# Gated delta-rule layer on one core: unnormalised keys and queries, with their sums of squares as token columns

## The chip, the cores and the metric

The kernel runs on one core of a Trainium2 chip. The core has TensorE (PE; its weight loads are shown as PEld), VectorE (DVE), ScalarE (ACT), GpSimd (POOL) and SyncE (SP), which starts the transfers. The metric is the device time of one execution in microseconds (us), less is better.

## The reference

Two layers work on 4 x 256 tokens of width 256: rotary attention with a routed feed-forward part (layer 0), then a gated delta rule with another feed-forward part (layer 1). The change lies in the delta rule. It has 16 key heads and 32 value heads (two value heads share a key head) of width 128:

```python
conv = sum((w[None, :, j:j + 1] * padded[:, :, j:j + T] for j in range(K)))
conv = jax.nn.silu(conv)
...
q = _l2norm(q)          # a / max(sqrt(sum(a*a)), 1e-12)
kk = _l2norm(kk)
beta = jax.nn.sigmoid(b_raw)
g = -jnp.exp(A_log) * jax.nn.softplus(a_raw + dt_bias)
decay = jnp.exp(g)
def step(state, inp):
    state = state * d_t[..., None, None]
    Sk = jnp.einsum('bhi,bhij->bhj', k_t, state)
    delta = (v_t - Sk) * b_t[..., None]
    state = state + jnp.einsum('bhi,bhj->bhij', k_t, delta)
    o = jnp.einsum('bhi,bhij->bhj', q_t, state)
...
y = o * jax.nn.silu(zz)
y = y * jax.lax.rsqrt(jnp.mean(y * y, axis=-1, keepdims=True) + 1e-06) * norm_w
out = jnp.einsum('btv,ov->bto', y.reshape(B, T, VDIM), W_out)
```

The kernel returns the residual stream after both layers.

## The kernel before

Everything is laid out by hand: each engine has its own program, and semaphores join them. Tokens are cut into 8 tiles of 128; a batch row has 256 tokens, two chunks of 128. Layer 1 starts with a norm, the decays' sums, the whole feed-forward part (`up`, `down`) and the preparation of head 0. Then `body(j, slot, i)` runs once for each of 16 key heads: heads 0, 1, 14 and 15 are written out and the rest is a loop of two heads. Within a body an engine works on head i and, in gaps that the lists `fill`, `mid`, `end` and `more` name, prepares head i + 1 and finishes the output of head i - 1.

One head goes through these stages.

- Products. TensorE turns V to token rows (`turn_v`, L764), ScalarE copies it (`copy_v`), GpSimd makes `Rb`, the bf16 copy of V's first chunk, in the first place of its body (`vb_done`, L1635). TensorE makes K K^T and K Q^T of every batch row (`products`, L777, L778). VectorE multiplies K K^T by the strict mask and by the decays (`matrices`, L1339, L1344, result N); ScalarE copies K Q^T (`copy_qk`, L1126) and GpSimd multiplies it by the decays (`decayed`, L1629). With them run z's gate (`tanh_z`, `gate_z`) and the sum of squares of the output of head i - 1 (`square_y`, `sum_y`, `mean_y`, then ScalarE's `scale_y`, Ln and Exp, L1169 and L1171), by which GpSimd scales y (`scale_y`, L1621).
- Inversion. ScalarE copies N to bf16 (Nb, L1132), TensorE turns TT (L815), and ScalarE copies the result (d_T, L1137). Then six levels (`LEVELS`) double the size of the inverted blocks: `corner` (L790), a masked copy by VectorE (L1363), `grow` (L800, L804), ScalarE's copies (L1145, L1149). Between them TensorE projects head i + 1 (`project`, L731), turns y (`turn_y`, L886) and projects the output (`project_out`, L897), and VectorE makes the convolution in steps of 128 x 1024 (`conv`, L1311). GpSimd adds the diagonal to N (L1649) and the mask to the next decays (`mask`, L1615).
- Solve. For two chunks c and three rounds a: `apply` (L840), `residual` (L852) or `link` (L860) on TensorE, `left_over` (L1377) and `update` (L1385) on VectorE.
- Output. `outputs` (L873 to L875), then `gate_o` (L1408).

Keys and queries of head i + 1 are normalised during the solve: ScalarE squares them (`square`), TensorE sums over the 128 partitions with a matrix of ones, so that the sum of a token stands in all partitions of a bank (`norms`, L751, banks 0 to 3), VectorE bounds it from below into `nrm` (`guard`, L1329, which increments `max_done`), ScalarE takes the power -1/2 as Ln and Exp (`rnorm`, L1096 and L1098), and VectorE multiplies (`unit`, L1335, which increments `kq_done`). `project_z` (L742) waits for `max_done`, since z's projection takes the same banks, and `products` waits for `kq_done`. `ACT_TABLE_LOAD` is put in by the compiler where ScalarE's next function is in another table.

## Time and profile before

| what | value |
|---|---|
| median of 3 runs | 1980.0 us (1975.21 to 1981.11) |
| profiled execution: time, span | 1971.39 us, 1969.4 us |
| busy: TensorE, VectorE, ScalarE, GpSimd | 89%, 77%, 62%, 32% |
| chain that ended last | PE 39%, DVE 12%, ACT 10%, issue 9%, POOL 2% |
| costliest group on VectorE | L1311, 192 instructions, 298.1 us |

The span is the time from the first to the last instruction of one profiled execution. Busy shares are shares of the span. The chain is followed back from the last instruction, at each step to what released it; the rest of it is time in between. Where a line of a timeline ends in brackets, the engine sat idle for so long before it, and the name is what released it.

### The profile page before, as it was taken

The page shows a single profiled execution, that of the slowest core. Times are in us where ns is not written, and L with a number is a line of the kernel's source. Part 1 is how long each engine was busy: PE and PEld are TensorE (multiplying, and loading weights), DVE is VectorE, ACT ScalarE, POOL GpSimd, SP SyncE. Part 2 cuts the span into 40 slices and gives each one's busy share as a digit, 9 for nine tenths or more (in the row PEclk, how much of TensorE's full clock was granted, in tenths as well). Part 3 has the DMA queues.
Part 4 walks back from the last instruction along what each step waited for, and adds up shares of the span by engine and source line. Part 5 has one row for each costly group of instructions (what it writes and reads, how often), then busy time and mean ns, then how long its engine had stood idle before and what let it go on. Part 6 is the DMA issues. An engine that isn't in the chain of part 4 may idle for free.

```text
span 1969.4 us, 35372 instructions
## 1 busy us (share of the span) xinstructions
PE 1749.0 (89%) x12824; PEld 1303.0 (66%) x12824; DVE 1519.3 (77%) x2421; ACT 1226.4 (62%) x2155; POOL 636.4 (32%) x442
## 2 busy tenths in 40 slices
PE   7899999999899778889888889888988888988976
PEld 5667676767657566667766667666776666756665
DVE  8788888888674787887777878778777787877853
ACT  3253534444355567777677877768767786777862
POOL 2212222231230535336053261432605326144140
PEclk9999999999999899999999999999999999999988
DMA  3011110101032001101101011010110101101000
GB/s 131 32 62 38 54 61 31 61 31 62 3 99 65 17 16 39 33 23 33 56 23 33 23 34 55 23 34 23 33 55 23 33 23 34 55 23 33 7 1 22
DMA packets 51465, 75.66 MB, mean 38 GB/s; under 512 B 3392, under 2 KB 41792, under 8 KB 51184
## 3 DMA queue, kind: packets, MB, share of 16 engines
q1 hardware_dynamic: 51312, 73.55, 11.7%
q8 instruction: 105, 1.72, 0.4%
q14 instruction: 48, 0.39, 0.1%
HBM read 72.29 MB, written 1.25 MB: 37 GB/s over the span
## 4 chain that ended last, share of the span: by engine, by line
PE 39%; DVE 12%; ACT 10%; issue 9%; POOL 2%; ACTq 0%; DVEq 0%; POOLq 0%
PE bank L897 6%; PE bank L731 6%; PE bank L852 5%; PE bank L742 4%; DVE d_sil L1311 4%; PE bank L790 2%; DVE d_Rb L1377 2%; PE bank L800 2%; PE bank L764 2%; POOL d_dec L1629 2%; DVE d_W L1385 2%; PE bank L873 1%; PE bank L875 1%; PE bank L874 1%; ACT d_TT L1149 1%
## 5 line engine op out<-in xcount | busy, mean ns | idle before, releaser
L1311 DVE SCALAR_TENSOR_TENSOR d_sil<-d_pre,d_w,d_sil 128x1024 f32<-128x1024 f32 x192 | 298.1, 1553 | 5.9 <-ACT d_pre L1081 5.6
L1635 POOL TENSOR_TENSOR d_Rb<-d_V,d_ones 128x512 bf16<-128x512 f32 x32 | 48.0, 1511 | 711.0 <-ACT d_V L1110 711.0
L1363 DVE CAST_PREDICATED d_X<-tables_sb,bank 128x512 bf16<-128x512 int32 x192 | 134.3, 700 | 147.6 <-PE bank L790 146.9
L731 PE MATMUL bank<-xnT,d_w 128*128 128x512 f32 x480 | 244.1, 644 | 0.8
L189 PE MATMUL bank<-xnT,a_w 128*128 128x512 f32 x512 | 237.0, 597 | 0.0
L1145 ACT ACTIVATE d_T<-bank 128x512 bf16<-128x512 f32 x160 | 98.5, 616 | 107.4 <-PE bank L800 105.1
L1629 POOL TENSOR_TENSOR d_dec<-d_dec,d_qk 128x384 f32<-128x384 f32 x128 | 133.2, 1064 | 44.2 <-DVE d_N L1344 44.2
L852 PEld LDWEIGHTS bank<-d_W,d_N 128*128 128x128 f32 x1024 | 122.7, 193 | 35.0 <-DVE d_W L1385 22.4
L189 PEld LDWEIGHTS bank<-xnT,a_w 128*128 128x128 f32 x512 | 90.9, 192 | 78.5 <-issue 78.5
L731 PEld LDWEIGHTS bank<-xnT,d_w 128*128 128x128 f32 x480 | 89.2, 202 | 79.3 <-issue 79.3
L489 POOL TENSOR_TENSOR a_hidc<-a_hid,a_comb 128x512 f32<-128x512 f32 x32 | 44.4, 1387 | 295.0 <-DVE a_hid L336 295.0
L852 PE MATMUL bank<-d_W,d_N 128*128 128x128 f32 x1024 | 129.6, 280 | 11.1 <-DVE d_W L1385 9.6
L742 PE MATMUL bank<-d_w,xnT 128*128 128x256 f32 x512 | 123.4, 384 | 12.0 <-DVE d_nrm L1329 12.0
L1377 DVE TENSOR_TENSOR d_Rb<-d_V,bank 128x512 bf16<-128x512 f32 x128 | 86.5, 685 | 56.9 <-PE bank L852 55.8
L897 PE MATMUL bank<-d_wo,d_yT 128*128 128x256 f32 x512 | 127.8, 394 | 0.9 <-ACT d_yT L1176 0.9
L508 ACT ACTIVATE a_sg<-a_sm 128x384 f32<-128x384 f32 x64 | 33.0, 515 | 151.9 <-DVE a_sm L341 151.9
L790 PE MATMUL bank<-d_T,d_Nb 128*128 128x64 bf16 x1536 | 79.2, 196 | 48.0 <-ACT d_T L1137 33.7
L1615 POOL TENSOR_TENSOR d_dec<-d_dec,tables_sb 128x512 f32<-128x512 f32 x64 | 116.6, 1850 | 16.2 <-DMA d_dec<-decay_scratch 16.2
L1649 POOL TENSOR_TENSOR d_N<-d_N,tables_sb 128x512 f32<-128x512 f32 x64 | 120.3, 1910 | 0.0
L1149 ACT ACTIVATE d_TT<-bank 128x512 bf16<-128x512 f32 x192 | 117.4, 611 | 4.5 <-PE bank L804 4.5
L790 PEld LDWEIGHTS bank<-d_T,d_Nb 128*128 128x128 bf16 x1536 | 65.0, 100 | 81.3 <-ACT d_T L1137 36.4
L481 POOL TENSOR_TENSOR a_qT<-a_rot_a,a_rot_b 128x512 f32<-128x512 f32 x64 | 81.2, 1270 | 100.4 <-DVE a_rot_b L325 100.4
(211 smaller groups left out, 4497.9 us busy)
## 6 DMA issues: line engine op xcount, KB each, us to landing
d_dec<-decay_scratch SPq DMA_DIRECT2D x32, 512.0 KB, 5.7
a_w<-w SPq DMA_DIRECT2D x16, 897.0 KB, 4.6
d_w<-w SPq DMA_DIRECT2D x16, 776.0 KB, 4.8
a_comb<-comb_scratch SPq DMA_DIRECT2D x16, 512.0 KB, 5.5
d_dec<-decay_scratch SPq DMA_DIRECT2D x32, 256.0 KB, 6.0
d_wo<-w SPq DMA_DIRECT2D x16, 256.0 KB, 3.0
f_w<-w SPq DMA_DIRECT2D x8, 256.0 KB, 3.7
tables_sb<-tables SPq DMA_DIRECT2D x1, 1056.0 KB, 8.4
```

Source lines behind the costliest of these rows:

```text
L189: last = pe.matmul(psum[bank][:, :], wq(slot, part, k), xnT[:, k, half * HALF:(half + 1) * HALF], start=(k == 0), stop=(k == KT - 1))
L731: last = pe.matmul(psum[bank][:, :], cols(slot, (c * KT + k) * P, P), xnT[:, k, h * HALF:(h + 1) * HALF], start=(k == 0), stop=(k == KT - 1))
L742: last = pe.matmul(psum[n][:, q * 2 * P:(q + 1) * 2 * P], xnT[:, k, t * P:(t + 1) * P], cols(slot, OZ + k * 2 * P, 2 * P), start=(k == 0), ...
L790: last = pe.matmul(psum[4 + 2 * v][:, n * 64:(n + 1) * 64], Nb[v][:, n // 2, n % 2, :], left(Tm[v][:, :, :], lv)[:, n], start=True, stop=True)
L852: last = pe.matmul(psum[5 + 2 * v][:, b * P:(b + 1) * P], N[v][:, b, 2 * c, :], Wv[v][:, b, c, :], start=True, stop=True)
L897: last = pe.matmul(psum[OUT_BANK[n]][:, q * D:(q + 1) * D], yT[v][:, t * P:(t + 1) * P], wo[slot][:, v, :], start=(v == 0), stop=(v == 1))
L1149: act.activation(right(TT[v][:, :, :], lv).rearrange("p n g w -> p (n g) w"), psum[4 + 2 * v][:, :].rearrange("p (a w) -> p a w", w=lv), A ...
L1311: dve.scalar_tensor_tensor(sil[c][:, :, :], pre[c % 2][:, :, tap:tap + S], cols(slot, OC + 4 * c + tap, 1), sil[c][:, :, :], ALU.mult, ALU ...
L1363: dve.copy_predicated(left(Xp[lv][:, v], lv), mask.unsqueeze(1).broadcast_to([P, 8, 64]).rearrange("p n (g w) -> p n g w", w=lv), psum[4 + ...
L1377: dve.tensor_tensor(Rb[v][:, :, :], V[v][:, :, c, :], psum[5 + 2 * v][:, :].rearrange("p (b d) -> p b d", b=B), ALU.add).then_inc(s["r_don ...
L1629: pool.tensor_tensor(g, g, qk[b % 2][:, :, :], ALU.mult).then_inc(s["p_done"], 1)
L1649: last = pool.tensor_tensor(n, n, tabs["neg_ident"].unsqueeze(1).broadcast_to([P, B, P]), ALU.add)
```

## The change

Keys and queries keep their length. With k = |k| k', the system for delta is the same when the columns of N and of the decayed K Q^T are divided by |k|^2 and V is multiplied by |k|; the length of q only scales the output, which a norm follows, so it goes into that norm's epsilon.

- The squares (`sq`) are now the stationary operand and one column of ones the moving one: 16 matmuls of one output column, all into bank 2, so a token's sum stands in its own partition.
- `guard` makes three columns of 8: `kss` (bounded sum of k), `qeps` (16e-6 times the bounded sum of q) and `krec`, the reciprocal of `kss`. It stands once in `end[3]`. `rnorm` and `unit` are gone. `key_norm`, a Sqrt on 8 columns, stands behind the last `copy_qk`.
- `copy_qk` and the first instruction of `matrices` are cut in two, for each chunk of keys has its own column of `krec`.
- GpSimd makes `Rb` as V times |k| and scales V in place, both behind `decayed(3)`; `apply` and the first `left_over` wait for them.
- `mean_y` adds `qeps` in place of 16e-6. `scale_y` on ScalarE becomes `root_y` (Sqrt), and the reciprocal, `inverse_y`, is VectorE's, behind `gate_z(3)` in level 0.

```diff
@@ -576,7 +576,11 @@
         gated = [m.sb(f"d_gated{h}", [P, 4, 2 * P]) for h in range(2)]
-        nrm = [m.sb(f"d_nrm{k}", [P, T]) for k in range(2)]
+        sq = [m.sb(f"d_sq{k}", [P, T]) for k in range(2)]
+        kss = m.sb("d_kss", [P, NT])
+        knorm = m.sb("d_knorm", [P, NT])
+        krec = m.sb("d_krec", [P, NT])
+        qeps = [m.sb(f"d_qeps{k}", [P, NT]) for k in range(2)]
         Xp = {lv: m.sb(f"d_X{lv}", [P, 2, 8, P], BF16) for lv in LEVELS}
...
@@ -733,7 +737,13 @@
             def project_z(slot, i, n):
-                pe.wait_ge(s["max_done"], i * 2 + n // 2 + 1)
+                if n < 2:
+                    pe.wait_ge(s["pre_done"], i * 8 + 5 + n)
+                    need(pe, s["acc_done"], (i - 2) * 4 + 3 + n)
+                elif n == 2:
+                    pe.wait_ge(s["kss_done"], i * 2 + 2)
+                else:
+                    pe.wait_ge(s["pre_done"], i * 8 + 8)
                 if isinstance(i, int) and i == 0 and n >= 2:
...
@@ -744,12 +754,14 @@
             def norms(i, c, h):
+
                 pe.wait_ge(s["sq_done"], i * 2 + c + 1)
-                pe.wait_ge(s["pre_done"], i * 8 + 4 + 2 * c + h + 1)
-                if c == 0:
-                    need(pe, s["acc_done"], (i - 2) * 4 + 2 + h + 1)
-                pe.matmul(psum[2 * c + h][:, :], onesf[:, :], nrm[c][:, h * HALF:(h + 1) * HALF],
-                          start=True, stop=True).then_inc(s["ssq_ready"], 1)
+                pe.wait_ge(s["pre_done"], i * 8 + 7)
+                for t in range(4 * h, 4 * h + 4):
+                    last = pe.matmul(psum[2][:, c * NT + t:c * NT + t + 1], sq[c][:, t * P:(t + 1) * P], onesf[:, 0:1],
+                                     start=True, stop=True)
+                if h:
+                    last.then_inc(s["ssq_ready"], 1)
...
@@ -831,7 +843,7 @@
                     pe.wait_ge(s["tt_done"], i * 12 + 11 + v)
-                    pe.wait_ge(s["vb_done"], i * 2 + v + 1)
+                    pe.wait_ge(s["vb_done"], i * 4 + 2 * v + 1)
                 elif k == 3:
...
@@ -902,7 +914,7 @@
                 project_z(slot, i, 2)
-                pe.wait_ge(s["kq_done"], i * 2 + 2)
+                pe.wait_ge(s["sil_done"], i * 4 + 2)
                 products(i, 0)
...
@@ -1035,12 +1036,13 @@
             down(2)
+            pe.wait_ge(ev["first_done"], 1)
             for h in range(2):
-                first_norms(0, h)
+                norms(0, 0, h)
             up(4)
             down(3)
             for h in range(2):
-                first_norms(1, h)
+                norms(0, 1, h)
             for u in range(5, UNITS):
...
@@ -1051,7 +1053,8 @@
                 else:
-                    pe.wait_ge(s["max_done"], 2)
+                    pe.wait_ge(s["kss_done"], 2)
+                    pe.wait_ge(s["pre_done"], 8)
                 for r in range(2):
...
@@ -1088,14 +1091,13 @@
                 act.wait_ge(s["sil_done"], i * 4 + c + 1)
-                act.activation(nrm[c][:, :], sil[c][:, :, :].rearrange("p b t -> p (b t)"), ACT.Square).then_inc(s["sq_done"], 1)
-
-            def rnorm(i, c):
-
-                act.wait_ge(s["max_done"], i * 2 + c + 1)
-                act.activation(nrm[c][:, :], nrm[c][:, :], ACT.Ln).then_inc(s["ln_done"], 1)
-                act.wait_ge(s["ln_done"], i * 2 + c + 1)
-                act.activation(nrm[c][:, :], nrm[c][:, :], ACT.Exp, scale=-0.5).then_inc(s["nrm_done"], 1)
+                act.activation(sq[c][:, :], sil[c][:, :, :].rearrange("p b t -> p (b t)"), ACT.Square).then_inc(s["sq_done"], 1)
+
+            def key_norm(i):
+
+                act.wait_ge(s["kss_done"], i * 2 + 1)
+                need(act, s["vb_done"], i * 4)
+                act.activation(knorm[:, :], kss[:, :], ACT.Sqrt).then_inc(s["knorm_done"], 1)
...
@@ -1123,8 +1125,11 @@
                     act.wait_ge(s["p_done"], i * 8 + 2 * (b - 2) + 2)
-                act.activation(qk[b % 2][:, :, :], psum[5 + 2 * (b % 2)][:, 0:3 * P].rearrange("p (c t) -> p c t", c=3),
-                               ACT.Copy).then_inc(s["qk_done"], 1)
+                act.wait_ge(s["krec_done"], i + 1)
+                ps = psum[5 + 2 * (b % 2)][:, 0:3 * P].rearrange("p (c t) -> p c t", c=3)
+                act.activation(qk[b % 2][:, 0:2, :], ps[:, 0:2, :], ACT.Copy, scale=krec[:, 2 * b:2 * b + 1])
+                act.activation(qk[b % 2][:, 2, :], ps[:, 2, :], ACT.Copy,
+                               scale=krec[:, 2 * b + 1:2 * b + 2]).then_inc(s["qk_done"], 1)
...
@@ -1164,11 +1169,9 @@
-            def scale_y(i):
+            def root_y(i):
                 act.wait_ge(s["yssm_done"], i + 1)
-                act.activation(yss[:, :, :], yss[:, :, :], ACT.Ln).then_inc(s["ysqrt_ln"], 1)
-                act.wait_ge(s["ysqrt_ln"], i + 1)
-                act.activation(yrs[:, :, :], yss[:, :, :], ACT.Exp, scale=-0.5).then_inc(s["yrs_done"], 1)
+                act.activation(yss[:, :, :], yss[:, :, :], ACT.Sqrt).then_inc(s["ystd_done"], 1)
...
@@ -1199,8 +1202,9 @@
                 copy_qk(i, 3)
+                key_norm(i)
                 if not first:
-                    scale_y(i - 1)
+                    root_y(i - 1)
                 fill = [([], []) for _ in LEVELS]
...
@@ -1233,8 +1237,6 @@
                     batch_decays(ni, ns, 3)
-                    rnorm(ni, 0)
-                    rnorm(ni, 1)
...
@@ -1322,22 +1322,24 @@
-            def guard(i, c, bank=0):
-                for h in range(2):
-                    dve.wait_ge(s["ssq_ready"], i * 4 + 2 * c + h + 1)
-
-                    last = dve.tensor_scalar(nrm[c][:, h * HALF:(h + 1) * HALF], psum[(bank or 2 * c) + h][:, :], 4e-24, None, ALU.max)
-                last.then_inc(s["max_done"], 1)
-
-            def unit(i, c):
-                dve.wait_ge(s["nrm_done"], i * 2 + c + 1)
-                f = sil[c][:, :, :].rearrange("p b t -> p (b t)")
-                dve.tensor_tensor(f, f, nrm[c][:, :], ALU.mult).then_inc(s["kq_done"], 1)
+            def guard(slot, i):
+                dve.wait_ge(s["ssq_ready"], i * 2 + 2)
+                need(dve, s["knorm_done"], i)
+                dve.tensor_scalar(kss[:, :], psum[2][:, NT:2 * NT], 4e-24, None, ALU.max).then_inc(s["kss_done"], 1)
+                dve.tensor_scalar(qeps[slot][:, :], psum[2][:, 0:NT], 4e-24, 16e-6, ALU.max, ALU.mult).then_inc(s["kss_done"], 1)
+                dve.wait_ge(s["kss_done"], i * 2 + 1)
+                need(dve, s["qk_done"], i * 4)
+                dve.reciprocal(krec[:, :], kss[:, :]).then_inc(s["krec_done"], 1)
             def matrices(i, slot, b):
                 dve.wait_ge(s["kk_ready"], i * 4 + b + 1)
-                dve.tensor_tensor(kk[b % 2][:, :, :], psum[4 + 2 * (b % 2)][:, 0:3 * P].rearrange("p (c t) -> p c t", c=3),
-                                  tabs["strict3"].rearrange("p (c t) -> p c t", c=3), ALU.mult).then_inc(s["kk_done"], 1)
+                dve.wait_ge(s["krec_done"], i + 1)
+                ps = psum[4 + 2 * (b % 2)][:, 0:3 * P].rearrange("p (c t) -> p c t", c=3)
+                strict = tabs["strict3"].rearrange("p (c t) -> p c t", c=3)
+                dve.scalar_tensor_tensor(kk[b % 2][:, 0:2, :], ps[:, 0:2, :], krec[:, 2 * b:2 * b + 1], strict[:, 0:2, :],
+                                         ALU.mult, ALU.mult)
+                dve.scalar_tensor_tensor(kk[b % 2][:, 2, :], ps[:, 2, :], krec[:, 2 * b + 1:2 * b + 2], strict[:, 2, :],
+                                         ALU.mult, ALU.mult).then_inc(s["kk_done"], 1)
                 dve.wait_ge(s["kk_done"], i * 4 + b + 1)
...
@@ -1374,6 +1376,8 @@
                 dve.wait_ge(s["resid_ready"], i * 10 + 2 * k + v + 1)
+                if c == 0 and a == 0:
+                    dve.wait_ge(s["vb_done"], i * 4 + 2 * v + 2)
                 dve.tensor_tensor(Rb[v][:, :, :], V[v][:, :, c, :], psum[5 + 2 * v][:, :].rearrange("p (b d) -> p b d", b=B),
...
@@ -1413,10 +1417,15 @@
-            def mean_y(i):
+            def mean_y(slot, i):
                 dve.wait_ge(s["yss_done"], i * 2 + 2)
-                dve.tensor_scalar(yss[:, :, :], yss[:, :, :], 1.0 / P, 16e-6, ALU.mult, ALU.add).then_inc(s["yssm_done"], 1)
+                dve.scalar_tensor_tensor(yss[:, :, :], yss[:, :, :], 1.0 / P, qeps[slot][:, :].unsqueeze(1).broadcast_to([P, 2, NT]),
+                                         ALU.mult, ALU.add).then_inc(s["yssm_done"], 1)
+
+            def inverse_y(i):
+                dve.wait_ge(s["ystd_done"], i + 1)
+                dve.reciprocal(yrs[:, :, :], yss[:, :, :]).then_inc(s["yrs_done"], 1)
...
@@ -1455,16 +1464,17 @@
                 if not first:
-                    mean_y(i - 1)
+                    mean_y(1 - slot, i - 1)
                 matrices(i, slot, 3)
                 fill = [([], []) for _ in LEVELS]
                 mid, end = [[] for _ in range(6)], [[] for _ in range(6)]
                 fill[0][0].append(lambda: gate_z(i, 3))
+                if not first:
+                    fill[0][0].append(lambda: inverse_y(i - 1))
                 if nxt:
                     nj, ns, ni = nxt
                     cv = lambda c, *steps: (lambda: conv(ns, ni, c, steps))
                     si = lambda c: (lambda: silu(ni, c))
-                    gd = lambda c: (lambda: guard(ni, c))
                     fill[0][0].append(lambda: columns(nj, ns, ni))
...
@@ -1477,9 +1487,8 @@
                     mid[2], end[2] = [cv(3, 1)], [cv(3, 2)]
-                    mid[3], end[3] = [si(2)], [gd(0)]
-                    mid[4], end[4] = [si(3)], [gd(1)]
-                    mid[5] = [lambda: unit(ni, 0)]
+                    mid[3], end[3] = [si(2)], [lambda: guard(ns, ni)]
+                    mid[4] = [si(3)]
                 if first:
...
@@ -1510,7 +1519,6 @@
                         plain(v)
-                    unit(ni, 1)
...
@@ -1600,7 +1605,8 @@
                 sum_y(LAST, v)
-            mean_y(LAST)
+            mean_y(LAST % 2, LAST)
+            inverse_y(LAST)
             for n in range(4):
...
@@ -1630,10 +1636,6 @@
                 nxt = after(j, slot, i)
-                for v in range(2):
-                    pool.wait_ge(s["v_done"], i * 4 + 2 * v + 2)
-                    pool.tensor_tensor(Rb[v][:, :, :], V[v][:, :, 0, :], onesf[:, :].unsqueeze(1).broadcast_to([P, B, P]),
-                                       ALU.mult).then_inc(s["vb_done"], 1)
                 decayed(i, slot, 0)
...
@@ -1641,6 +1643,13 @@
                 decayed(i, slot, 3)
+                pool.wait_ge(s["knorm_done"], i + 1)
+                scale = knorm[:, :].rearrange("p (b c) -> p b c", c=2).unsqueeze(3).broadcast_to([P, B, 2, P])
+                for v in range(2):
+                    pool.wait_ge(s["v_done"], i * 4 + 2 * v + 2)
+                    pool.tensor_tensor(Rb[v][:, :, :], V[v][:, :, 0, :], scale[:, :, 0, :], ALU.mult).then_inc(s["vb_done"], 1)
+                    pool.wait_ge(s["vb_done"], i * 4 + 2 * v + 1)
+                    pool.tensor_tensor(V[v][:, :, :, :], V[v][:, :, :, :], scale, ALU.mult).then_inc(s["vb_done"], 1)
                 for v in range(2):
                     pool.wait_ge(s["nb_done"], i * 2 + v + 1)
                     pool.wait_ge(s["tt1_done"], i * 2 + v + 1)
```

## Rows read from the trace of the kernel before

**Rows 1.** The page: busy time, share of the span and instructions of each engine.

```profile
PE 1749.0 (89%) x12824; PEld 1303.0 (66%) x12824; DVE 1519.3 (77%) x2421; ACT 1226.4 (62%) x2155; POOL 636.4 (32%) x442
```

**Rows 2.** Timeline of TensorE in one head: start, us, instructions, idle time before.

```profile
1239.84 0.41 PE L790 MATMUL bank<-d_T,d_Nb 128*128 128x64 bf16 x8 [2.32 <-ACT d_T L1137]
...
1241.94 3.64 PE L731 MATMUL bank<-xnT,d_w 128*128 128x512 f32 x4
...
1247.57 1.07 PE L886 MATMUL bank<-tables_sb,x_sb 128*128 128x128 f32 x8
...
1251.98 1.95 PE L731 MATMUL bank<-xnT,d_w 128*128 128x512 f32 x4
...
1269.66 0.40 PE L840 MATMUL bank<-d_Rb,d_TT 128*128 128x128 bf16 x4 [0.47 <-ACT d_TT L1149]
...
1271.67 1.95 PE L852 MATMUL bank<-d_W,d_N 128*128 128x128 f32 x16
...
1278.08 1.02 PE L751 MATMUL bank<-d_nrm,d_ones 128*128 128x512 f32 x2
...
1289.14 1.99 PE L742 MATMUL bank<-d_w,xnT 128*128 128x256 f32 x8 [0.80 <-DVE d_nrm L1329]
...
1290.97 1.95 PE L852 MATMUL bank<-d_W,d_N 128*128 128x128 f32 x16
```

**Rows 3.** Waits from 640 to 1900 us: who waited for whom, total, times, longest.

```profile
PE bank L742 <- DVE d_nrm L1329: 12.0, 15, 0.8
```

**Rows 4.** Timeline of VectorE in the same head.

```profile
1252.60 2.39 DVE L1311 SCALAR_TENSOR_TENSOR d_sil<-d_pre,d_w,d_sil 128x1024 f32<-128x1024 f32 x1
...
1276.65 1.28 DVE L1311 SCALAR_TENSOR_TENSOR d_sil<-d_pre,d_w,d_sil 128x1024 f32<-128x1024 f32 x1
...
1287.80 1.28 DVE L1329 TENSOR_SCALAR d_nrm<-bank 128x512 f32<-128x512 f32 x2
```

**Rows 5.** Groups by line, whole span: shapes, count, busy us, mean ns, idle before.

```profile
L1096 ACT ACT_TABLE_LOAD x32 | 41.1, 1283 | 0.6
...
L1096 ACT ACTIVATE d_nrm<-d_nrm 128x1024 f32<-128x1024 f32 x32 | 33.8, 1057 | 0.4
...
L1118 ACT ACTIVATE d_dec<-d_dec,d_gcol 128x256 f32<-128x256 f32 (+1 forms) x256 | 94.4, 442 | 0.0
...
L1126 ACT ACTIVATE d_qk<-bank 128x384 f32<-128x384 f32 x64 | 31.0, 485 | 29.5 <-POOL d_dec L1629 27.3 <-PE bank L778 2.2
...
L1419 DVE TENSOR_SCALAR d_yss<-d_yss 128x16 f32<-128x16 f32 x16 | 2.7, 166 | 0.0
...
L1621 POOL TENSOR_TENSOR x_sb<-x_sb,d_yrs 128x1024 f32<-128x1024 f32 x32 | 60.4, 1906 | 101.1 <-ACT d_yrs L1171 101.1
```

**Rows 6.** The router's matmuls, L309: durations min/median/max, first and last start.

```profile
L309 PE MATMUL bank<-r_w,xnT x32: 173/256/256, 19.8 to 23.2; 128*128 128x8 f32 x32
```

**Rows 7.** Timeline of ScalarE in the same head.

```profile
1232.37 0.49 ACT L1126 ACTIVATE d_qk<-bank 128x384 f32<-128x384 f32 x1 [1.72 <-POOL d_dec L1629]
...
1235.82 1.99 ACT L1132 ACTIVATE d_Nb<-d_N 128x1024 bf16<-128x1024 f32 x2
...
1266.57 1.06 ACT L1086 ACTIVATE d_yT<-d_sil 128x1024 f32<-128x1024 f32 x1 [1.02 <-PE bank L897]
```

**Rows 8.** Timeline of ScalarE behind the last head.

```profile
1944.25 1.28 ACT L1169 ACT_TABLE_LOAD   x1
...
1945.72 0.22 ACT L1169 ACTIVATE d_yss<-d_yss 128x16 f32<-128x16 f32 x1 [0.19 <-DVE d_yss L1419]
```

**Rows 9.** Timeline of GpSimd in the same head, and in the last head.

```profile
1243.54 7.91 POOL L1649 TENSOR_TENSOR d_N<-d_N,tables_sb 128x512 f32<-128x512 f32 x4
...
1251.41 6.93 POOL L1615 TENSOR_TENSOR d_dec<-d_dec,tables_sb 128x512 f32<-128x512 f32 x4
...
1896.85 4.98 POOL L1649 TENSOR_TENSOR d_N<-d_N,tables_sb 128x512 f32<-128x512 f32 x4
```

**Rows 10.** A stretch: length, busy us by engine, granted clock, DMA share, GB/s.

```profile
1242.00:1244.00 2.00, 2.00 (x7) 0.97 (x4) 2.00 (x3) 0.73 (x2) 2.00 (x3) 0.50 0.00 0
```

24 lines of the change are left out of this document (5 added, 19 removed).

## The prediction

> **What bounds the kernel.** I read the page first, then the groups by line, the waits, and the timelines of one steady head of layer 1 engine by engine. TensorE is busy 89% of the span [rows 1], so a saving on another engine counts only where TensorE stands still for it. Everything the change touches lies in layer 1 with its 16 heads. In the timeline of one head the reader is to see three kinds of stretch. In most of the inversion TensorE runs on, and other engines' work is free. At the start of the inversion ScalarE is the last link: the first product waits 2.32 us for the copy of d_T [rows 2]. In the solve VectorE and TensorE answer each other, and one wait there belongs to the normalisation: z's projection waits 0.80 us for the guard [rows 2], in 15 heads, 12.0 us in all [rows 3].
>
> **Solve stage, per head.** Four guards and two products with the norm leave VectorE: two pairs of 1.28, as the one at 1287.80, and two instructions on 1024 columns, each about a convolution step alone, 1.28 [rows 4], 5.1 us. Most of it buys nothing. The products with the norm fall before the last gating and after `plain`, where VectorE would only wait for TensorE. The first guard pair is what z's projection waits for. Three instructions on 8 columns replace it. The nearest row is `mean_y` on 16 columns, 166 ns [rows 5], so some 0.4 us, and the projection no longer waits for them: banks 0 and 1 hold no sums any more. TensorE gains its whole wait, 0.80 us. The next lateness is TensorE itself: projection and residual follow one another, 1289.14 and 1290.97 [rows 2], so the second guard's end gives nothing. TensorE's norms: before, four fp32 matmuls of 512 columns, two records each, one such pair 1.02 us from start to end at 1278.08 [rows 2], up to 4 us per head. Now 16 of one column, 32 records. The router's 32 records of 8 columns ran from 19.8 to 23.2 [rows 6], 0.11 us each, so 3.5 us: equal. Three of the four calls lie where TensorE waits for VectorE or ScalarE anyway. The bounds are -0.1 and +0.3 us; I take 0.
>
> **ScalarE.** Out go two Ln/Exp pairs on 1024 columns, each instruction 1057 ns and each behind a table load of 1283 ns [rows 5]: 9.4 us per head, at the very end of the head, after which ScalarE waited for TensorE: 0 on the path. `scale_y` is different. It lies between `copy_qk` and the Nb copy. From the end of `copy_qk` at 1232.86 to Nb at 1235.82 are 2.96 us [rows 7], two loads and two small instructions. Now one load (Sqrt) serves `key_norm` and `root_y`: 1.28 and two small ones of (2.96 - 2.57) / 2 = 0.2, 1.7 us, a gain of 1.25. Against it: `copy_qk` is cut in two with a scale column. The nearest pair, 256 and 128 columns in the decays with a mean of 442, against 485 for one [rows 5], gives +0.40 at most; with the overlap of neighbours I take +0.3. VectorE's `matrices` is cut likewise. A cut adds the fixed part of one instruction, at most `mean_y`'s 166 ns [rows 5]; I take +0.13. Two of these stand before the last `copy_qk` (it waits for `decayed(1)`, that for N): +0.26 and its own +0.3. The gain is 1.25 - 0.56 = 0.7 us per head (bounds 0 and 1.25). The transposes behind the projections come some 0.4 us later, still before the d_T copy wants them.
>
> After Sqrt, Tanh needs its table again: a load of 1.28 in front of `tanh_in` in level 5. At the end of the kernel the load starts at 1944.25, although its activation waited until 1945.72 for VectorE [rows 8]: a load does not wait for the semaphore. Before L1086 ScalarE was idle 1.02 us [rows 7]. So 0.27 us are exposed, passed on through d_TT to `apply`; the whole 1.28 is the upper bound. The Trainium skill (ScalarE: Activation LUTs, What ACT_TABLE_LOAD costs) adds a drain of 1.38 us to every load; the rows show none, as two loads fit in the gap before Nb. By the page the load saved would be worth 2.66 and the forecast about 20 us lower, unless the load added in level 5 takes that back.
>
> **GpSimd** loses its place in time. `vb_done` leaves the start of the head, where it ran under other work, and comes back behind `decayed(3)` with the scaling of V, 1024 columns in place, twice, beside it. The broadcast along the last axis is `scale_y`'s, 1.9 us for 1024 [rows 5]; so 2 x (1.5 + 1.9) = 6.8 us. Also `yrs` is now made by a VectorE reciprocal behind the first copy of level 0 and the gating. It is ready at about 1241 instead of before Nb at 1235.8, 5 us later. `decayed(2)`, `decayed(3)`, the diagonal and the mask shift by 5 + 6.8, some 12 us: the diagonal's end from 1251.4 to about 1263, the mask's from 1258.3 to about 1270 [rows 9]. The residual wants the diagonal at 1271.67 [rows 2], 1270 when TensorE has gained, and ScalarE the mask at about 1273. Slack 7 and 3 us: nothing waits. `turn_y` at 1247.57 [rows 2] needs the first scaled half and gets it at about 1244: also free. VectorE's reciprocal is one small instruction.
>
> The shared cost is another. The convolution step takes 2.39 us at 1252.60, beside GpSimd's mask, and 1.28 at 1276.65, alone [rows 4]; the diagonal's four took 7.91 us there and 4.98 in the last head, which has no convolutions [rows 9]. The scaling of y ran in a hole of VectorE and now falls on convolutions, and the mask comes up to the solve. In most of this time TensorE is the bound; I take +0.3 us per head (bounds 0 and +2). The Trainium skill (GPSIMD Engine Reference, Specifications) says that the two engines share the SBUF interface, with contention for VectorE instructions with two SBUF inputs. The rows agree, and this is the rule that speaks against the change.
>
> **Clock.** After TensorE's short idle times at the start of the inversion the granted clock was 0.50 from 1242 to 1244, the lower level, 1.2 GHz [rows 10]; four records of L731 took 3.64 us there and 1.95 at full clock [rows 2]: 1.7 us lost. Eight heads of the inversion show this; the others have about the same idle time at full clock, so it is at the edge. The 2.32 us shrink by 0.7 + 0.4 to about 1.2. I expect most falls to go: 5 of 8, 8 us. Bounds: all go, 13 us gained; or all 15 heads fall, 12 us lost.
>
> **Sum.** Per head -0.80 - 0.7 + 0.27 + 0.3 = -0.93; over 15 heads -14. Head 0 has no `scale_y` and so pays a load and the longer pieces, +2. The tail saves one load and has a reciprocal instead of Exp, -1.2. Before the heads TensorE is full and the norms cost the same, 0; the clock -8. Together -21. The profiled execution took 1971.4 us (span 1969.4 and 2.0 around it), which becomes 1950. It lies 8.6 below the median of the runs, 1980.0; the change of -21 set against that median gives 1959.
>
> **Rivals.** A, nothing gained: the table load is exposed in full, and the split pieces cost their upper bounds. Then -0.80 - 0.5 + 1.28 + 0.3 = +0.3 per head, 4 in all, and the clock brings back some 5: 1980. For it: TensorE already waits 0.47 us for d_TT at `apply` [rows 2]. Against: the early load [rows 8]. B, the other side: GpSimd becomes the bound. Its work from y's scaling to the first half of the diagonal must fit in 29 us (1241 to 1270). Uncontended that is 3.8 + 3.9 + 2.6 + 3.8 + 2.5 = 16.6; all slowed by 7.91 / 4.98 = 1.6, 26; if scaling V goes at the mask's rate, 6.93 / 4 for 512 columns [rows 9], 29. From there the residual waits, and the mask runs into the solve, where VectorE paces TensorE: two convolutions 1.1 slower each, +2.2, and a wait of up to 1; with 1.2 gained elsewhere +2 per head, +30, 2010. C: the removed VectorE and ScalarE work counts more, half of the 5.1 us: -2.6 more per head, 1920; the idle time that follows it speaks against this.
>
> **Chances.** Forecast case 0.73, A 0.13, B 0.10, C 0.04. A measurement here can tell 0.3%, 6 us, from no change. The forecast case runs from 1943 (clock all gained, no contention) to 1976 (clock unchanged, contention 0.8 per head) and leaves about 0.04 within 0.3%; A gives mostly same. Faster 0.73, same 0.14, slower 0.13. The range for 8 in 10 is 1942 to 1984, A included.
>
> **What would show it.** Right: no wait of L742 for VectorE in the solve; two table loads per head instead of six; Nb 1.2 us nearer to the end of `copy_qk`; the wait for d_T at the start of the inversion under 1.6 us; fewer L731 groups above 3 us. Wrong: TensorE or ScalarE waiting for d_N, d_dec or x_sb from GpSimd; convolutions above 2 us inside the solve; a wait for d_TT above 1 us at `apply`.

## The result and the profile after

The changed kernel takes 1997.0 us (median of 4 runs, 1992.6 to 2000.3) against 1977.6 us for the kernel before in the same session (1971.0 to 1981.1): ratio 1.0102, 95% interval 1.0077 to 1.0128. The forecast was 1959, with 0.73 on faster: it is slower, outside the range, and by none of the rivals. The profiled execution spans 1990.3 us where that of before spans 1969.4, 20.9 more. Runs 3 and 12 below had one execution each far above their others (2982 and 2462 us), which the ranges given leave out.

The page of the changed kernel, to be read beside [rows 1]:

```profile
PE 1778.5 (89%) x13208; PEld 1379.0 (69%) x13208; DVE 1488.4 (75%) x2453; ACT 1089.6 (55%) x2090; POOL 730.2 (37%) x474
...
PE 43%; DVE 13%; ACT 9%; issue 7%; DVEq 0%; POOL 0%; ACTq 0%; POOLq 0%
```

VectorE lost 31 us of work and ScalarE 137, as the diff says. GpSimd gained 94. TensorE did the same matrix products, apart from the sums, and is busy 30 us longer. The same work in more time points at its clock (mean granted clock 0.952 here, 0.971 before).

Where it went is found by cutting each head at five starts in TensorE's timeline: V is turned (L776, before L764), TT is turned (L827, L815), first product of the inversion (L802, L790), first `apply` (L852, L840), first product of the output (L885, L873). Means over heads 1 to 14, in us; the last column is from one head's start to the next:

| kernel | products | TT to first product | inversion | solve | head |
|---|---|---|---|---|---|
| before | 16.60 | 3.36 | 28.41 | 26.91 | 81.49 |
| after | 16.92 | 2.36 | 29.44 | 28.18 | 83.08 |
| difference | +0.32 | -1.00 | +1.03 | +1.27 | +1.59 |

Fourteen heads make +22 of the 21 us; head 0 pays 0.7 more with its lead, the last head with the tail gives 2.0 back.

A head's stage has one length at full clock and a longer one when the clock falls in it, and the two are easily told apart: in the kernel before the inversion takes 27.5 in six of these heads and 28.9 to 30.0 in the other eight, and the products 16.03, or 17.6 to 17.7 in five heads, all where the loop of two heads begins a new turn. In the changed kernel the products take 16.46, or 18.1 in four heads, the inversion 28.70 once and 29.3 to 29.9 in 13 heads, and all 14 solves take 27.6 us or more (one 31.4), with a stretch at the lower clock in each. Timeline of TensorE in one solve of the changed kernel, and the windows over it (length, busy us by engine, granted clock, DMA share, GB/s):

```profile
1290.33 1.01 PE L761 MATMUL bank<-d_ones,d_sq 128*128 128x1 f32 x8
1291.88 2.05 PE L864 MATMUL bank<-d_W,d_N 128*128 128x128 f32 x16 [0.55 <-DVE d_W L1389]
1293.77 0.95 PE L761 MATMUL bank<-d_ones,d_sq 128*128 128x1 f32 x8
1294.58 0.69 PE L852 MATMUL bank<-d_Rb,d_TT 128*128 128x128 bf16 x8
1295.11 1.00 PE L761 MATMUL bank<-d_ones,d_sq 128*128 128x1 f32 x8
1296.67 3.68 PE L872 MATMUL bank<-d_W,d_N 128*128 128x128 f32 x16 [0.55 <-DVE d_W L1389]
```

```profile
1292.00:1296.00 4.00, 4.00 (x40) 3.92 (x40) 4.00 (x6) 2.35 (x6) 0.00 (x0) 1.00 0.00 0
1296.00:1300.00 4.00, 3.45 (x18) 3.36 (x18) 3.10 (x5) 0.67 (x2) 0.00 (x0) 0.60 0.02 4
```

The reader is to see that `link` (L872) takes 3.68 us for the sixteen matmuls for which `residual` (L864) takes 2.05, and that the granted clock, at 1.00 until then, averages 0.60 there: most of these 4 us lie at the lower level, 1.2 GHz. `link` is the longer one in 13 of the 14 heads; in one (solve 27.6) the low stretch lies beside it. What TensorE did just before is three groups of the new sums, 128 x 1. By group, whole span:

```profile
L761 PE MATMUL bank<-d_ones,d_sq 128*128 128x1 f32 x512 | 68.4, 255 | 0.3 <-ACT d_sq L1094 0.3
L872 PE MATMUL bank<-d_W,d_N 128*128 128x128 f32 x256 | 54.0, 397 | 10.3 <-DVE d_W L1389 10.2
```

In the kernel before the group that answers to L872 has the same count and a mean of 289 ns instead of 397.

ScalarE and VectorE at the end of the inversion, and the product that follows on TensorE:

```profile
1281.03 1.28 ACT L1089 ACT_TABLE_LOAD   x1 [1.00 <-PE bank L909]
1282.33 1.06 ACT L1089 ACTIVATE d_yT<-d_sil 128x1024 f32<-128x1024 f32 x1
...
1284.72 0.58 ACT L1154 ACTIVATE d_TT<-bank 128x512 bf16<-128x512 f32 x1
```

```profile
1283.42 4.00 DVE L1317 SCALAR_TENSOR_TENSOR d_sil<-d_yT,d_sil 128x1024 f32<-128x1024 f32 x2 [0.47 <-ACT d_yT L1089]
```

```profile
1254.40 0.41 PE L802 MATMUL bank<-d_T,d_Nb 128*128 128x64 bf16 x8 [1.31 <-ACT d_T L1142]
...
1257.01 3.06 PE L735 MATMUL bank<-xnT,d_w 128*128 128x512 f32 x4
...
1285.36 0.40 PE L852 MATMUL bank<-d_Rb,d_TT 128*128 128x128 bf16 x4 [1.03 <-ACT d_TT L1154]
```

The new table load started only after ScalarE's idle time behind L909, not in it, and the second `apply` waits 1.03 us for d_TT, which stood behind the load; it was 0.47 before [rows 2]. The wait at the start of the inversion fell from 2.32 [rows 2] to 1.31, yet the projection behind it took 3.06 us for four records, 1.95 at full clock [rows 2]. So it was in the other heads: 16 loads at L1089, with 14.3 us of idle time before them. And GpSimd in the same head:

```profile
1256.51 4.73 POOL L1627 TENSOR_TENSOR x_sb<-x_sb,d_yrs 128x1024 f32<-128x1024 f32 x2 [8.70 <-DVE d_yrs L1428]
...
1268.16 2.76 POOL L1652 TENSOR_TENSOR d_V<-d_V,d_knorm 128x1024 f32<-128x1024 f32 x1
...
1275.71 4.96 POOL L1658 TENSOR_TENSOR d_N<-d_N,tables_sb 128x512 f32<-128x512 f32 x4
1280.64 7.91 POOL L1621 TENSOR_TENSOR d_dec<-d_dec,tables_sb 128x512 f32<-128x512 f32 x4
```

Its chain ends at 1288.55, 4.6 us after the solve began (1283.92), where it had ended at 1258.34, 11 us ahead of the `apply` at 1269.66 [rows 2, 9]. No group of TensorE waits for GpSimd or for z's guard any more.

### The profile page after: what moved, and what is told of

It is laid out like the page before. It is cut to its first block, busy times and chain, and to the rows that moved or that the text cites. A ratio compares the mean times of both kernels' runs of the same rounds, so it can differ in the third digit from the quotient of the medians.

```text
span 1990.3 us, 36376 instructions
## 1 busy us (share of the span) xinstructions
PE 1778.5 (89%) x13208; PEld 1379.0 (69%) x13208; DVE 1488.4 (75%) x2453; ACT 1089.6 (55%) x2090; POOL 730.2 (37%) x474
## 4 chain that ended last, share of the span: by engine, by line
PE 43%; DVE 13%; ACT 9%; issue 7%; DVEq 0%; POOL 0%; ACTq 0%; POOLq 0%
PE bank L735 6%; PE bank L909 6%; PE bank L864 5%; PE bank L752 4%; PE bank L872 2%; PE bank L802 2%; DVE d_sil L1311 2%; DVE d_Rb L1381 2%; PE bank L812 2%; DVE d_N L1346 2%; ACT d_TT L1154 2%; PE bank L816 1%; DVE d_yss L1418 1%; PE bank L776 1%; PE bank L885 1%
## 5 line engine op out<-in xcount | busy, mean ns | idle before, releaser
L1635 POOL TENSOR_TENSOR d_dec<-d_dec,d_qk 128x384 f32<-128x384 f32 x128 | 160.6, 1278 | 626.4 <-DVE d_N L1346 626.4
L1311 DVE SCALAR_TENSOR_TENSOR d_sil<-d_pre,d_w,d_sil 128x1024 f32<-128x1024 f32 x192 | 301.2, 1568 | 5.0 <-ACT d_pre L1084 4.7
L864 PE MATMUL bank<-d_W,d_N 128*128 128x128 f32 x1024 | 134.6, 287 | 12.8 <-DVE d_W L1389 10.7
L864 PEld LDWEIGHTS bank<-d_W,d_N 128*128 128x128 f32 x1024 | 127.5, 200 | 25.8 <-DVE d_W L1389 12.3
L1112 ACT ACTIVATE d_V<-bank 128x512 f32<-128x512 f32 x64 | 35.2, 609 | 193.9 <-PE bank L776 193.9
L1627 POOL TENSOR_TENSOR x_sb<-x_sb,d_yrs 128x1024 f32<-128x1024 f32 x32 | 73.7, 2325 | 165.1 <-DVE d_yrs L1428 165.1
L1621 POOL TENSOR_TENSOR d_dec<-d_dec,tables_sb 128x512 f32<-128x512 f32 x64 | 122.7, 1946 | 15.8 <-DMA d_dec<-decay_scratch 15.8
L909 PE MATMUL bank<-d_wo,d_yT 128*128 128x256 f32 x512 | 127.1, 393 | 0.9 <-ACT d_yT L1179 0.9
L852 PE MATMUL bank<-d_Rb,d_TT 128*128 128x128 bf16 x768 | 75.7, 225 | 54.0 <-DVE d_Rb L1381 25.9
L802 PE MATMUL bank<-d_T,d_Nb 128*128 128x64 bf16 x1536 | 81.0, 198 | 33.3 <-ACT d_T L1142 18.4
```

What stands on the lines that cost most here:

```text
L802: last = pe.matmul(psum[4 + 2 * v][:, n * 64:(n + 1) * 64], Nb[v][:, n // 2, n % 2, :], left(Tm[v][:, :, :], lv)[:, n], start=True, stop=True)
L864: last = pe.matmul(psum[5 + 2 * v][:, b * P:(b + 1) * P], N[v][:, b, 2 * c, :], Wv[v][:, b, c, :], start=True, stop=True)
L909: last = pe.matmul(psum[OUT_BANK[n]][:, q * D:(q + 1) * D], yT[v][:, t * P:(t + 1) * P], wo[slot][:, v, :], start=(v == 0), stop=(v == 1))
L1311: dve.scalar_tensor_tensor(sil[c][:, :, :], pre[c % 2][:, :, tap:tap + S], cols(slot, OC + 4 * c + tap, 1), sil[c][:, :, :], ALU.mult, ALU ...
L1621: last = pool.tensor_tensor(g, g, tabs["future"].unsqueeze(1).broadcast_to([P, B, P]), ALU.add)
L1635: pool.tensor_tensor(g, g, qk[b % 2][:, :, :], ALU.mult).then_inc(s["p_done"], 1)
```

## The experiments

Two theories stood against each other at first: the clock falls because of the one-column sums, or because of the shorter and later waits that the change makes; and beside them the late table load and GpSimd as the slower engine. Stage lengths are means over heads 1 to 14, as above; "full" is the length that a stage shows again and again where the clock does not fall in it. The runs fell into five sessions, in which the kernel before had medians of 1973.5 to 1979.8; ratios are against the same session.

**1. Wide sums.** The changed kernel, with 128 columns of ones in place of one in the new sums.

```diff
-last = pe.matmul(psum[2][:, c * NT + t:c * NT + t + 1], sq[c][:, t * P:(t + 1) * P], onesf[:, 0:1],
+last = pe.matmul(psum[2][:, c * NT + t:c * NT + t + P], sq[c][:, t * P:(t + 1) * P], onesf[:, :],
```

> The changed kernel with one edit: the column of ones that the squares multiply is 128 columns wide, so the same number of matmuls and weight loads, with more columns in each; bank 2 keeps the same 16 sums. Clock theory: in the changed kernel the granted clock falls in the solve in 14 of 16 heads, where TensorE has only one-column matmuls between its waits, and each fall costs link some 1.6 us. With wide matmuls link goes back to 2.05 us in most heads and the time falls by 15 to 25 us, to about 1975. Rival, GpSimd: the moved scaling of V and y costs the time by contention with VectorE; then this edit changes nothing, 1997 within 5, or adds a little for the columns.

Measured: 1960.6 us, ratio to before 0.991 (0.9875 to 0.9943), 36 us less than the changed kernel. Its solve takes 26.48 or 26.49 us in each of the 14 heads. Timeline of TensorE in one of them:

```profile
1273.84 1.06 PE L761 MATMUL bank<-d_ones,d_sq 128*128 128x128 f32 x8
1274.73 0.61 PE L852 MATMUL bank<-d_Rb,d_TT 128*128 128x128 bf16 x8
1275.18 1.11 PE L761 MATMUL bank<-d_ones,d_sq 128*128 128x128 f32 x8
1276.73 2.05 PE L872 MATMUL bank<-d_W,d_N 128*128 128x128 f32 x16 [0.45 <-DVE d_W L1389]
```

The wide groups take 1.06 to 1.11 us, the narrow ones 0.95 to 1.01: 128 times the columns for a tenth more time, and `link` is back at 2.05. The number of matmuls and weight loads is the same, so this is shown: with the narrow shape of the sums the solve loses its clock, with the wide one it keeps it. The inversion falls less often too: 28.97 on average, 28.70 in ten heads.

**2. Early table.** The changed kernel, with a Tanh of one column in level 4, which brings the table load forward to where ScalarE has room.

```diff
+fill[4][1].append(lambda: act.activation(warm[:, :], onesf[:, 0:1], ACT.Tanh))
 fill[5][0].append(lambda: tanh_in(ni, 0))
```

> The changed kernel with one edit: a Tanh on one column, without a wait, stands before the copies of level 4, where ScalarE is idle 1.2 to 1.7 us, so that the Tanh table is there when tanh_in comes. Load theory: the load costs apply some 1.0 to 1.3 us per head, and this gives 12 to 18 us back, to about 1982; the wait of L852 for d_TT falls from 1.03 to about 0.47 us. Rival, GpSimd or the clock alone: below 5 us.

Measured: 1970.4 us, 0.996 (0.9944 to 0.9977). The inversion at full clock becomes 28.06. The clock still falls in the solve, but in seven heads instead of 14 (27.7 to 31.0 us): the width of the sums is not all that decides how often. The gain of 27 us is above the 12 to 18 expected, since falls went too.

**3. Both.**

> Both edits, wide sums and the early table load. If both theories hold and add, 1997 less 20 less 15, about 1962, below the kernel before and near the forecast. If the one hides behind the other, about 1975. Rival, GpSimd: no less than 1990.

Measured: 1945.8 us (1944.7 to 1946.3), 0.983 (0.9787 to 0.9872). Inversion 28.10, solve 26.39. Between run 2 and this one only the width of the sums differs: no solve falls, and the time is 25 us less. From the first run the inversion at full clock went from 28.70 to 28.06: the late load costs 0.64 us per head. The two repairs are worth 51 us together.

**4. The kernel before, with narrow sums.** The other direction: its sums over 16 columns instead of 512. The kernel leaves out the rest of the norms, so its output is not right, and the guard's bound is 1.

```diff
-pe.matmul(psum[2 * c + h][:, :], onesf[:, :], nrm[c][:, h * HALF:(h + 1) * HALF],
+pe.matmul(psum[2 * c + h][:, 0:16], onesf[:, :], nrm[c][:, h * HALF:h * HALF + 16],
```

> The kernel before with its sums of squares cut from 512 output columns to 16 (timing only: the norms are not computed, and the guard's bound is 1, so that stale columns do no harm). TensorE has 3 us per head less to do. Clock theory: the clock now falls in the solve of the kernel before as well, link goes from 2.05 to about 3.6 us in most heads, and the time rises by 10 to 25 us though work was taken away. Rival: less work on TensorE, the time is the same or falls by up to 10 us.

Measured: 1995.1 us, 1.0089 (1.0062 to 1.0116). Less work of TensorE, 16 us more time. The solve, 26.91 in every head of the kernel before, is now 26.91 in three heads and 27.7 to 30.3 in the rest. `link` takes 2.8 to 3.2 us in seven heads and 2.05 in the others, whose falls lie elsewhere in the solve; the inversion has heads with two falls (30.0). So such falls come without the rest of the change. But this run does not separate the shape from the time: a pair of sums takes 0.35 us instead of 1.02 to 1.08, and TensorE's wait before `link` doubles, from 10.4 us in all to 21.1. What changes the shape alone are run 1, run 3 against run 2, and run 17 against run 14. Groups by line:

```profile
L751 PE MATMUL bank<-d_nrm,d_ones 128*128 128x16 f32 x120 | 21.3, 254 | 0.3 <-ACT d_nrm L1091 0.3
L860 PE MATMUL bank<-d_W,d_N 128*128 128x128 f32 x256 | 41.7, 330 | 21.1 <-DVE d_W L1385 21.1
```

**5 and 6. Filling the wait before the first product.** Matmuls of ones on ones (128 x 128, into bank 6, which is overwritten afterwards) where TensorE waits for d_T: five in the kernel of run 3, eight in the kernel before.

```diff
+for _ in range(5):
+    pe.matmul(psum[6][:, 0:P], onesf[:, :], onesf[:, :], start=True, stop=True)
 for li in range(len(LEVELS)):
     corner(li, 0)
```

> Both edits and, between the transposes and the first product of the inversion, five matmuls of ones by ones (1.1 us) into a bank that is free then; TensorE is idle there for 1.3 us. Clock theory: the falls of the clock at the start of the inversion go too, 2 to 4 heads still have one in the run without, so 3 to 8 us less, about 1941. Rival: those matmuls delay the first product, or the clock has another cause, 1946 or a few us more.

> The kernel before with eight matmuls of ones by ones (1.8 us) in its idle 2.32 us before the first product of the inversion, and nothing else. Clock theory: its falls of the clock there, in 7 or 8 heads at 1.7 us each, go, so 10 to 15 us less, about 1966, though no work was taken away. Rival, the clock has another cause: 1979, or more if the matmuls are in the way.

Measured: 1943.2 us, 0.9847 (0.9823 to 0.9871), and 1966.7 us, 0.9968 (0.9947 to 0.9989). In both, no inversion of heads 1 to 14 falls any more: 28.06 and 27.49. In the kernel before this took 0.9 us per head from the inversion and put 0.6 on the products (17.18; where the loop of heads begins a new turn, 18.3 to 20.8), so 7 us are left. The clock is not what took them: it falls at two of the five turns, where it fell at all five before. At each of the five TensorE now stands idle once more behind the turn of V, with no releaser ("issue"), and why was not tried:

```profile
PE bank L742 <- issue: 11.4, 5, 2.6
```

**7, 8 and 10. Single costs.** The kernel of run 3 without most of V's scaling; with the pieces of `copy_qk` and `matrices` in one instruction again, for which both chunks take the first one's reciprocal (in these two the output is not right); and with z's first two projections waiting for `kss_done` again.

```diff
-pool.tensor_tensor(V[v][:, :, :, :], V[v][:, :, :, :], scale, ALU.mult)
+pool.tensor_tensor(V[v][:, :, :, 0:1], V[v][:, :, :, 0:1], scale[:, :, :, 0:1], ALU.mult)
```

```diff
-act.activation(qk[b % 2][:, 0:2, :], ps[:, 0:2, :], ACT.Copy, scale=krec[:, 2 * b:2 * b + 1])
-act.activation(qk[b % 2][:, 2, :], ps[:, 2, :], ACT.Copy,
-               scale=krec[:, 2 * b + 1:2 * b + 2]).then_inc(s["qk_done"], 1)
+act.activation(qk[b % 2][:, :, :], ps, ACT.Copy, scale=krec[:, 2 * b:2 * b + 1]).then_inc(s["qk_done"], 1)
```

```diff
 if n < 2:
+    pe.wait_ge(s["kss_done"], i * 2 + 2)
     pe.wait_ge(s["pre_done"], i * 8 + 5 + n)
```

> Both edits, and GpSimd scales one column of V in place of all (timing only, V stays unscaled). It takes 2 x 2.5 us per head from GpSimd and brings the mask out of the first round of the solve. Forecast's term: contention is worth 0.3 us per head, so 0 to 8 us less than 1946. Rival B, GpSimd decides: over 15 us less.

> Both edits, and copy_qk and the first instruction of matrices stay whole, with the first chunk's reciprocal for both chunks (timing only, the second chunk's scale is wrong). The forecast put 0.56 us per head on the split pieces, so 6 to 10 us less than 1946. The stage from the turned V to the transposes should fall from 16.66 to 16.2 us. Rival: the pieces are hidden, under 3 us.

> Both edits, and z's first projections wait for the small guard again, as they did for the large one. If the forecast's 0.80 us per head was the wait itself, this costs what the small guard takes, about 0.4 us per head plus its semaphores, 5 to 8 us more than 1946, and the solve rises from 26.39 to about 26.8 us. If the banks did not matter, no change.

Measured: 1944.8, 1941.9 and 1945.9 us against 1945.8; ratios 0.985, 0.9839 and 0.9827 against 0.983. Scaling V costs the solve 0.5 us per head (26.39 to 25.90), but the clock then fell at the loop's turn in five heads instead of two (products 17.03 for 16.66), and the time stayed. The pieces cost 0.28 us in the products at full clock (16.46 to 16.18) and 0.23 behind them (2.36 to 2.13); all but 4 us of these 7 went to the clock again. The gate costs nothing (solve 26.35): the three small instructions are early enough.

**9. Only the Sqrt.** The kernel before, keys and queries normalised as ever, with just `root_y` and `inverse_y` of the change and the early Tanh.

```diff
-act.activation(yss[:, :, :], yss[:, :, :], ACT.Ln).then_inc(s["ysqrt_ln"], 1)
-act.wait_ge(s["ysqrt_ln"], i + 1)
-act.activation(yrs[:, :, :], yss[:, :, :], ACT.Exp, scale=-0.5).then_inc(s["yrs_done"], 1)
+act.activation(yss[:, :, :], yss[:, :, :], ACT.Sqrt).then_inc(s["ysqrt_ln"], 1)
```

> One part alone on the kernel before: y's Ln and Exp become a Sqrt and a VectorE reciprocal in the changed kernel's place, with the early Tanh. Forecast's term: a table load and a small instruction less between copy_qk and Nb, 1.3 to 1.5 us per head off the wait of the first product for d_T, and nothing else: 15 x 1.3 = 20 us less, about 1958, more if falls of the clock go with the wait. Rival: the wait falls but is given back in the inversion, which TensorE paces: under 8 us.

Measured: 1941.3 us, 0.9811 (0.978 to 0.9842). Products 16.01, TT to first product 2.04, inversion 28.36 (28.06 full), solve 27.01. One part of the change gives as much as the repaired whole, and the 28.06 stands here too, against 27.52 before: whatever gives 0.54 back in the inversion came in with this part, not with V.

**11. GpSimd in another order.** Runs 3 and 5, with `decayed(2)`, `decayed(3)` and V's first half before y's scaling.

> Both edits and the five matmuls of the idle time, and GpSimd does decayed(2), decayed(3), vb and V of the first value head before it scales y, in the 8 us in which it waits for the reciprocal. GpSimd's mask then ends before the solve. From 1943 another 0 to 8 us less, about 1939; rival: y's scaling comes too late for turn_y, a few us more than 1943.

Measured: 1968.9 us, 0.9947 (0.9925 to 0.9969): 26 us worse than run 5. Products 17.53 and TT to first product 3.27. Waits of TensorE from 640 to 1900 us, and the masked copy of TT by VectorE, in run 5 and here:

```profile
PE bank L828 <- DVE d_TT L1362: 31.6, 32, 5.9
...
L1362 DVE CAST_PREDICATED d_TT<-tables_sb,d_N 128x512 bf16<-128x512 int32 x32 | 23.4, 788 | 0.0
...
L1362 DVE CAST_PREDICATED d_TT<-tables_sb,d_N 128x512 bf16<-128x512 int32 x32 | 47.3, 1530 | 0.0
```

GpSimd's early work now falls beside the masked copy of N into TT, which takes 1530 ns instead of 788 while the instructions of `matrices` before it keep their length (571 and 573 ns at L1350), and TensorE waits for VectorE. The solve did come to 25.90: the order helps where it was meant to, and costs more where it was not.

**12, 13 and 15. The reciprocal earlier.** `inverse_y` behind the two copies of TT, where VectorE has nothing to do, instead of behind the first masked copy and the gating: in the kernel of run 3, in that of run 9, and in the changed kernel alone.

```diff
-if not first:
-    fill[0][0].append(lambda: inverse_y(i - 1))
...
-invert(i, fill)
+invert(i, fill, [] if first else [lambda: inverse_y(i - 1)])
```

> The kernel with the wide ones column and the early Tanh, and VectorE's reciprocal for y (inverse_y) moved from behind gate_z(3) and the first masked copy of level 0 to the place behind the two copies of TT, before the first level, where VectorE is idle. Theory (y's scaling on GpSimd, made late by the reciprocal, falls beside the convolutions and pushes the mask into the solve): the scaling starts some 4 us earlier, the inversion goes from 28.1 to about 27.5 us at full clock and the solve from 26.4 to about 25.9, some 15 us in all: about 1931. Rival (the inversion's 0.5 us come from the shorter idle time at its start, after which other work becomes the bound): 1943 to 1948, no change beyond 0.3%.

> The kernel before with the Sqrt and VectorE's reciprocal for y, the early Tanh, and the reciprocal behind the copies of TT as in the run beside it; keys and queries are normalised as before. If y's scaling lay too late there too, the inversion goes from 28.1-28.4 to 27.5 us: about 1931 to 1933. If not: 1941 as without the move. It also tells whether anything of the unnormalised keys and queries is worth having: the two kernels with the move differ then only by them.

> The changed kernel with the reciprocal moved to the place behind the copies of TT, alone. Theory (two separate losses): the 0.5 us of the inversion and 0.5 of the solve come back, 15 us less, but the falls of the granted clock in the solve (13 to 14 of 16 heads) stay, since its sums are still 128 x 1 matmuls: about 1982, link groups above 3.5 us in 13 or more heads. Rival (the falls in the solve come from lateness of GpSimd's mask and go with it): link groups at 2.05 us, about 1965.

Measured: 1946.7 us, 0.9831 (0.9764 to 0.9899); 1944.1 us, 0.9826 (0.9774 to 0.9878); 1998.6 us, 1.0103 (1.0068 to 1.0139). The mechanism was there, and the time did not move. Timeline of GpSimd in one head of run 12, which starts at 1210.67, and under it the same lines of run 3, where that head starts at 1209.94:

```profile
1227.38 3.75 POOL L1629 TENSOR_TENSOR x_sb<-x_sb,d_yrs 128x1024 f32<-128x1024 f32 x2 [4.48 <-DVE d_yrs L1432]
...
1251.79 5.96 POOL L1623 TENSOR_TENSOR d_dec<-d_dec,tables_sb 128x512 f32<-128x512 f32 x4
```

```profile
1230.86 4.73 POOL L1629 TENSOR_TENSOR x_sb<-x_sb,d_yrs 128x1024 f32<-128x1024 f32 x2 [8.70 <-DVE d_yrs L1430]
...
1256.05 6.93 POOL L1623 TENSOR_TENSOR d_dec<-d_dec,tables_sb 128x512 f32<-128x512 f32 x4
```

VectorE in the same two heads, run 12 first:

```profile
1232.67 1.47 DVE L1313 SCALAR_TENSOR_TENSOR d_sil<-d_pre,d_w,d_sil 128x1024 f32<-128x1024 f32 x1
...
1256.48 3.47 DVE L1319 SCALAR_TENSOR_TENSOR d_sil<-d_yT,d_sil 128x1024 f32<-128x1024 f32 x2
```

```profile
1231.77 2.06 DVE L1313 SCALAR_TENSOR_TENSOR d_sil<-d_pre,d_w,d_sil 128x1024 f32<-128x1024 f32 x1
...
1256.30 4.32 DVE L1319 SCALAR_TENSOR_TENSOR d_sil<-d_yT,d_sil 128x1024 f32<-128x1024 f32 x2
```

Counted from the head's start, y's scaling begins at 16.7 us instead of 20.9 and no longer lies beside a convolution, the first convolution takes 1.47 us instead of 2.06, and the gated pair at the start of the solve 3.47 instead of 4.32. What counts is who waits: VectorE's convolutions take no less time in all (304.0 us in run 3, 307.2 in run 12), but TensorE's waits for VectorE's masked copies in the inversion fall by 10 us. Run 3, then run 12, whole span:

```profile
PE bank L813 <- DVE d_X L1367: 43.5, 61, 1.7
...
PE bank L813 <- DVE d_X L1369: 33.5, 42, 1.7
```

At full clock the inversion goes from 28.06 to 27.26 in both kernels, and in run 12 the solve goes from 26.41 to 25.90: 1.3 us per head, 18 in all. But in seven of 14 heads of run 12 the inversion took 29.57, with a fall behind the same 1.31 us wait that run 3 had passed 13 times of 14 at full clock, and the products fell three times instead of twice. In run 13 too seven inversions fell (29.2), where run 9 had five. In run 15 the falls in the solve stayed, as the first theory said (13 of 14 solves above 26.48 us, mean 28.93), though `link` was above 3.5 us in seven heads and not in 13. My 1982 was missed because the falls were deeper: the inversion fell in eleven heads instead of 13, but to 30.2 or more over 27.9 at full clock, and the solve lost 0.75 us more per head than in the changed kernel.

**14. The reciprocal earlier and the wait filled.** Run 12 with four of the matmuls of run 5.

> As the first, and four matmuls of ones on ones (128 x 128, into bank 6, which the corners overwrite) before the first corner, where TensorE waits for d_T. Theory (the falls of the granted clock that are left in the inversion follow that wait): no fall in the inversion, 2 to 4 us less than the first, about 1928. Rival (falls are gone already, or go elsewhere): as the first or up to 3 us more.

Measured: 1922.6 us (1920.9 to 1925.3), 0.971 (0.9659 to 0.9761), the fastest of all: 74 us below the changed kernel, 52 below the kernel before in that session (1974.8). In heads 1 to 14 every inversion takes 27.26 to 27.29, every solve 25.89 or 25.90, every products stage 16.37 to 16.46. TensorE in one head:

```profile
1218.06 1.06 PE L828 MATMUL bank<-d_identb,d_TT 128*128 128x128 bf16 x16
1218.95 1.11 PE L831 MATMUL bank<-d_ones 128*128 128x128 f32 x8
1220.42 0.41 PE L803 MATMUL bank<-d_T,d_Nb 128*128 128x64 bf16 x8 [0.36 <-ACT d_T L1145]
```

The fill takes nothing from anyone: the first product comes 2.36 us after TT's turn as it did without it; of the wait of 1.31 us 0.36 is left.

**16. The same additions without the change.** The kernel of run 13 with the four matmuls.

> The kernel before (keys and queries normalised) with all three additions of the fastest kernel so far: Sqrt and VectorE's reciprocal for y with the reciprocal behind the copies of TT, the early Tanh, and four matmuls of ones before the first corner. Theory (the additions carry the gain; the unnormalised keys and queries add 1 us per head in the solve and take 0.7 back in the products): no falls in the inversion, 27.3 us there, 16.0, 2.0 and 27.0 in the other three stages, head 78.6, about 1930: 0.4% behind the fastest kernel. Rival (the unnormalised form is what makes it fast): 1940 or more. Rival (it costs): 1922 or less.

Measured: 1926.7 us (1924.3 to 1932.1), 0.9741 (0.9716 to 0.9767). Products 16.41 (falls at the loop's turn in three heads), 2.04, inversion 27.27, solve 27.00. So the unnormalised keys and queries are worth 1.1 us per head in the solve and cost 0.7 in the two stages before the inversion; the two kernels, 0.971 and 0.9741 of before with intervals that overlap, are not told apart.

**17. The fastest kernel with one-column sums.** Run 14, but `onesf[:, 0:1]` and one output column, as in the changed kernel.

> The fastest kernel so far (early reciprocal, early Tanh, four matmuls of ones), but with its sums as in the changed kernel, one column of ones and 128 x 1 matmuls. Theory (those matmuls bring the clock down in the solve wherever they stand): link groups at 3.5 us or more in at least 10 heads, solve 28 us instead of 25.9, 30 us more, about 1953. Rival (with the inversion at full clock the solve keeps it too): within 5 us of 1923.

Measured: 1960.3 us (1956.7 to 1971.2), 0.9926 (0.9899 to 0.9954), 38 more than run 14. All inversions are at full clock (27.26), four solves too (25.90), and ten take 27.0 to 32.0; `link` takes over 3.5 us in six heads, where ten were expected. TensorE in one of these, and its windows:

```profile
1106.03 1.01 PE L762 MATMUL bank<-d_ones,d_sq 128*128 128x1 f32 x8
1107.59 2.89 PE L867 MATMUL bank<-d_W,d_N 128*128 128x128 f32 x16 [0.55 <-DVE d_W L1395]
1110.27 1.71 PE L762 MATMUL bank<-d_ones,d_sq 128*128 128x1 f32 x8
1111.84 1.01 PE L855 MATMUL bank<-d_Rb,d_TT 128*128 128x128 bf16 x8
1112.64 1.81 PE L762 MATMUL bank<-d_ones,d_sq 128*128 128x1 f32 x8
1114.32 3.76 PE L875 MATMUL bank<-d_W,d_N 128*128 128x128 f32 x16
```

```profile
1104.00:1108.00 4.00, 2.96 (x29) 2.62 (x28) 3.63 (x5) 3.71 (x7) 0.00 (x0) 1.00 0.00 0
1108.00:1112.00 4.00, 4.00 (x25) 4.00 (x24) 3.41 (x5) 2.44 (x5) 0.00 (x0) 0.57 0.00 0
1112.00:1116.00 4.00, 4.00 (x24) 4.00 (x23) 2.88 (x4) 0.00 (x0) 0.00 (x0) 0.50 0.02 4
```

With a stage at full clock ahead of it, and with the rest of the kernel the same to the instruction, the one column alone costs 2%. At the lower level a group of eight takes 1.7 to 1.8 us instead of 1.0, and in five of the ten heads 13 us or more of the solve lie at that level. That the slowed narrow groups hold it there is a guess.

## Why the prediction was wrong

Against the profiled execution the forecast was -21 us, measured is +21: a miss of 42. Some 28 of it lie in the clock and 16 in the sum at full clock; the ends outside heads 1 to 14 give 2 back.

**The step that failed first** is the clock, and with it the line on the norms, "16 of one column, 32 records ... so 3.5 us: equal". In duration this was right: eight records took 1.01 us against the 0.9 that follows from the router's 0.11 each. But I asked of the new sums only how long they take, and of the clock only what it does in the inversion, whose falls the rows of before showed. The solve, which had kept full clock in all these heads, was not on the list of places where it could fall, neither in the sum nor in the rivals. There it fell in all 14: 28.18 against the 26.48 of run 1, 1.70 per head, 24 us. Three pairs that differ in nothing but the width of the sums show the cause: the changed kernel and run 1, runs 2 and 3, runs 17 and 14 (36, 25 and 38 us). Run 4 shows such falls in the kernel before as well, but there the waits grew too.

**The other half of the clock term**, 5 of 8 falls in the inversion to go because its first wait shrinks to about 1.2 us, failed too. The wait shrank to 1.31, but 13 heads instead of eight fell, less deep: 0.74 us per head over the full 28.70 where before had 0.89 over 27.52, -2 us instead of -8. Four falls at the loop's turn instead of five give another -1. So the clock gave +20 where the sum had -8.

**The sum at full clock**, against before, per head, the changed kernel's lengths taken from run 1:

| step | forecast | measured | from |
|---|---|---|---|
| Sqrt for Ln and Exp, less the cut pieces | -0.70 | -0.57 | first product 1.00 earlier, products 16.46 for 16.03 |
| Tanh's load | +0.27 | +0.64 | runs 1 and 3 |
| solve, the wait for z's guard | -0.80 | -1.01 | 25.90 in runs 7, 12 and 14 for 26.91 |
| GpSimd beside VectorE | +0.30 | +1.12 | inversion 28.06 for 27.52, solve 26.48 for 25.90 |
| together | -0.93 | +0.18 | |

- Sqrt for Ln and Exp: right. By run 8 the cut pieces cost 0.51 us, for which the forecast had 0.56.
- The load. "A load does not wait for the semaphore" was read from one place [rows 8] and carried to another. At L1089 it began after a wait of 1.00 us for L909. I had taken the whole of ScalarE's idle time as its cover [rows 7], and it covered next to nothing. The upper bound was 1.28; the measured 0.64 is half of it. Why a load runs ahead in one place and not in the other was not tried; two semaphores are waited for before L1089 and one in the tail. The drain that the Trainium skill (ScalarE: Activation LUTs, What ACT_TABLE_LOAD costs) adds to a load is not in the trace here either: the load of 1281.03 ends at 1282.31 and its activation starts at 1282.33.
- The solve. The wait of L742 is gone, as forecast, and nothing that late came in its place. Not for the reason given first, though, that banks 0 and 1 hold no sums any more: run 10 puts the wait for the guard back and pays nothing, so it is the short guard that frees the projection.
- GpSimd. The order and most of the lateness were foreseen (12 us): counted from the head's start (1220.43 before, 1235.58 after), the diagonal ends at 45.1 us instead of 31.0 and the mask at 53.0 instead of 37.9. What was not foreseen is the price on VectorE: no wait for GpSimd appeared, but the convolution beside y's scaling took 2.06 instead of 1.47 (run 3 against run 12), and the mask ran 4.6 us into the solve, where the gated pair took 4.00. Runs 7 and 12 show the two parts. The convolutions did not get slower on the whole (1553 ns on average before, 1568 after); other ones are slow now, and TensorE waits for those. The gated pair did, from 1216 ns for one to 1584. The Trainium skill (GPSIMD Engine Reference, Specifications) names this contention, and the trace agrees; the forecast priced it at a quarter of what it came to. Rival B, GpSimd as the bound, did not occur; its 29 us, on which its condition rests, do not come out of its terms either (16.6 less V's 3.8, slowed by 1.6, and 6.93 for V are 27).
- Rival A had the load's exposure right as a mechanism and half its size.

**What is left open.** Why the same wait of 1.31 us is followed by a fall in 1 of 14 heads in run 3 and in 7 of 14 in run 12. Repairs that made other stages shorter were partly taken back by falls elsewhere (runs 7, 8, 12), until the last wait was filled as well (run 14); in run 6 an idle time at the loop's turn took the gain back, not the clock. What it is about the narrow sums that brings the clock down, their few columns or something that goes with them, is not shown either. So the price of a wait in this kernel is not a constant, and a sum of parts over one trace does not give it. That the falls follow where the pieces land in time is a guess.

## What to carry to other kernels

Ask of every matmul put into a stretch with little slack not only how long it takes but what it does to TensorE's clock: here sums with one output column took nearly the time of sums with 128 and cost 2% of the kernel, and widening them cost 0.1 us for eight records. Where a wait of 1 to 2 us comes back in every head, throwaway matmuls in it can be worth more than the wait itself, if the clock falls behind it: 24 us for 4 matmuls per head from run 12, where it fell in seven heads, to run 14, and 3 us from run 3, where it fell in one, to run 5. Cut a change into its parts before it is kept: one part of this one, the Sqrt, reached 1926.7 us with the same additions with which the whole reached 1922.6.

## What the runs showed of the hardware

- A group of eight fp32 records takes 0.95 to 1.01 us with one output column and 1.06 to 1.11 with 128, and in heads 1 to 14 only the kernels with narrow ones had falls of the granted clock in the solve (0.50 to 0.60 over 4 us, `link` at 3.68 to 3.76 us instead of 2.05). The written-out head 0 has them in the kernel before too.
- A table load of ScalarE took 1.28 us everywhere. It ran ahead of its activation's wait in one place [rows 8] and began only after an idle 1.00 us in another.
- The gated pair of VectorE took 3.47 to 4.32 us where GpSimd's mask ran beside it for part or all of the time; its two instructions had a mean of 1.22 us each in the kernel before. The masked copy of N into TT took 0.79 us, and 1.53 where GpSimd worked beside it (run 11). The mask took 5.96, 6.93 or 7.91 us for the same four instructions.
